# Attention with 32-wide heads in chunks of four heads, packed by way of DRAM, in a two-layer decoder

## What is computed

```python
q = q.reshape(B, S, 16, 32); k = k.reshape(B, M, 16, 32); v = v.reshape(B, M, 16, 32)
scores = einsum('bqhd,bkhd->bhqk', q, k) / sqrt(32)     # causal mask in the self-attentions
o = einsum('bhqk,bkhd->bqhd', softmax(scores), v)
```

## Time and profile before

| | us |
|---|---|
| median of three runs | 3690.84 (3683.32 to 3691.17) |
| the profiled execution | 3685.6, its span 3683.8 |
| granted TensorE clock over the span | 0.875 of full speed |
| busy PE / DVE / ACT / POOL | 3145.7 / 1262.7 / 966.9 / 835.5 |

### The profile page before, as it was taken

How to read it: one execution, slowest core, us unless ns; L and a number is a source line. 1 busy time by engine, 2 the same in 40 slices (tenths; PEclk the granted TensorE clock), 3 DMA queues, 4 the chain that set the end, 5 groups by cost and what they waited for, 6 DMA issues and landing times. The chain is left out here.

```text
span 3683.8 us, 40622 instructions
## 1 busy us (share of the span) xinstructions
PE 3145.7 (85%) x13163; PEld 1907.7 (52%) x13166; DVE 1262.7 (34%) x1863; ACT 966.9 (26%) x2096; POOL 835.5 (23%) x819
## 2 busy tenths in 40 slices
PE   7699796988549786888996998999999856999997
PEld 3354342333548633446885884555554442777773
DVE  3133334564401212435434225555552131111114
ACT  1133033554101012323332004444442000222220
POOL 2100001100121101002442104555553013212215
PEclk9656897999669986659998999999999957999998
DMA  2132203331059612313443433222220000999996
GB/s 77 44 80 58 88 12 76 71 76 31 28 183 325 225 62 58 81 47 123 140 142 114 133 99 132 71 71 72 71 71 20 24 18 16 340 334 338 338 332 190
DMA packets 320633, 442.93 MB, mean 120 GB/s; under 512 B 45502, under 2 KB 179622, under 8 KB 320520
## 3 DMA queue, kind: packets, MB, share of 16 engines
q1 hardware_dynamic: 290056, 370.14, 32.4%
q0 software_dynamic: 15488, 44.09, 3.8%
q10 hardware_dynamic: 14976, 27.27, 2.1%
HBM read 308.78 MB, written 75.58 MB: 104 GB/s over the span
## 5 line engine op out<-in xcount | busy, mean ns | idle before, releaser
L1360 PE MATMUL ps<-moe_blocks_xgt,moe_blocks_w 128*128 128x128 f32 (+1 forms) x3072 | 364.0, 277 | 8.8 <-DMA moe_blocks_b1s<-rb_cols 5.5
L510 ACT ACTIVATE normed<-ps 128x512 f32<-128x512 f32 (+3 forms) x512 | 247.5, 516 | 463.7 <-PE ps L452 293.3
L1360 PEld LDWEIGHTS ps<-moe_blocks_xgt,moe_blocks_w 128*128 128x128 f32 (+1 forms) x3072 | 348.9, 183 | 16.6 <-issue 15.0
L2239 POOL TENSOR_TENSOR normed<-normed,xa_core_rinv 128x257 f32<-128x257 f32 (+1 forms) x256 | 266.2, 1062 | 273.0 <-DVE xa_core_rinv L2170 273.0
L1342 PE MATMUL ps<-moe_blocks_w,moe_blocks_ht 128*128 128x512 f32 (+1 forms) x624 | 284.9, 593 | 0.0
L2206 ACT ACTIVATE normed<-ps,xa_core_nmax 128x257 f32<-128x257 f32 (+1 forms) x256 | 173.8, 685 | 321.8 <-DVE xa_core_nmax L2165 321.4
L2116 PE MATMUL ps<-xa_core_k,xa_core_q 128*128 128x512 f32 x512 | 242.3, 596 | 14.1 <-DVE xa_core_k L2155 11.4
L2165 DVE TENSOR_REDUCE xa_core_nmax<-ps 128x1 f32<-128x257 f32 (+1 forms) x256 | 164.5, 683 | 250.1 <-PE ps L2116 250.1
L1431 DVE COPY moe_blocks_y<-ps 128x512 f32<-128x512 f32 x104 | 72.0, 692 | 459.9 <-PE ps L1342 436.3
L2142 PE MATMUL ps<-xa_core_pt,xa_core_v 128*128 128x512 f32 x512 | 225.1, 592 | 0.7 <-DVE xa_core_pt L2178 0.7
L559 DVE TENSOR_REDUCE xa_core_nmax<-ps 128x1 f32<-128x1024 f32 x128 | 156.0, 1224 | 139.9 <-PE ps L432 139.9
(11 more groups left out here) (290 smaller groups left out, 5263.7 us busy)
## 6 DMA issues: line engine op xcount, KB each, us to landing
moe_blocks_w<-L_ffn_rw SPq DMA_DIRECT2D x80, 704.0 KB
moe_blocks_w<-L_ffn_rw SPq DMA_DIRECT2D x80, 512.0 KB
...
moe_y<-moe_blocks_y ACTq DMA_DIRECT2D x104, 256.0 KB
sa_core_packed<-sa_core_parts SPq DMA_DIRECT2D x384, 64.0 KB
k_raw<-xa_kq_raw SPq DMA_DIRECT2D x64, 256.0 KB, 2.0
v_rows<-normed SPq DMA_DIRECT2D x64, 256.0 KB
...
```

Of the source, the lines that this page charges most:

```text
L510: nc.scalar.activation(probs[:, e % RING, a:S], g.ps[:, 4 + h, a:S], ACT.Exp).then_inc(exp_done, 1)
L1360: mm = nc.tensor.matmul(g.ps[0:fn, 2 + s % 2 + 2 * half, f * P:(f + 1) * P], w1s[s][:, k, half * F + f0:half * F + f0 + fn], xgt[:, s % 2, ...
L2239: ins = nc.gpsimd.tensor_tensor(prob[:, n % PR, lo:hi], prob[:, n % PR, lo:hi], rinv[:, n % PR, m:m + 1].to_broadcast([P, hi - lo]), ALU.mult)
```

## The change

Only `attention_core` and the layout of v change. The work goes in 8 **chunks** i of four heads, one for each unit.

- **Packing.** `spill(i)` writes all parts of a unit to a DRAM buffer in one transfer (128 rows of 8 KB in sa, 12 KB in xa), and `pack(i)` waits for it and reads them back in six transfers, each 32 rows of 4 heads, into `pq` and `pk`. There are three slots in place of four for pairs. SP's order is `spill(i + 2)`, `pack(i + 2)`, `put_rows(i + 1)`; `put_rows` has two transfers for four heads. At the start the order is spill 0, spill 1, pack 0, pack 1.
- **High parts.** ACT makes those of unit i + 2 in step nkt / 2 of chunk i.
- **Values.** Four matmuls with 32 columns of v write the four quarters of PSUM bank 6, in the rows of the output, and four with 32 columns of ones write the sums to bank 7. `take` copies both banks straight to `total` and `ot`; `osb` and `lay` are gone. v is stored without ones, and the POOL memsets of ones in v are gone.
- **Order on PE.** A step makes scores of heads 0 and 1, up to three pieces of chunk i + 1 (eight pieces a chunk in sa, sixteen in xa), scores of heads 2 and 3, and the values of the step before. The pieces now run one chunk ahead. In sa two score matmuls stand together and then their two masks. Row maxima are turned in the last step of a chunk.
- **DVE.** `norm(i - 1)` comes after the piece PCS // 2 of chunk i + 1 and waits for `take` alone.

```diff
-    packed = st.sbuf("packed", [P, SLOTS, 2, 1 + KB, S], F32R)
+    pq = st.sbuf("pq", [P, SLOTS, HPC, S], F32R)
+    pk = st.sbuf("pk", [P, SLOTS, HPC, KB * S], F32R)
+    parts_dram = nc.dram_tensor(st.name + "_parts_rows", (NI, P, 2 + 2 * KB, S), F32, kind="Internal").ap()
...
+    nmax = st.sbuf("nmax", [P, 2, HPC * QB])
+    rows = st.sbuf("rows", [HPC * QB, 2, 2, P], F32R)
...
-            def pack(j):
-                u, s = j // 2, j % SLOTS
-                sp.wait_ge(low_done, 2 * u + 2)
-                if j >= SLOTS:
-                    sp.wait_ge(st_made, 2 * nkt * (j - SLOTS + 1))
-                t = parts[u % PB]
-                for h in range(2):
-                    a = (2 * (j % 2) + h) * DH
-                    for r, (qp, kp) in enumerate(TERMS):
-                        sp.dma_start(packed[r * DH:(r + 1) * DH, s, h, 0, :].bitcast(F32),
-                                     t[a:a + DH, qp, :].bitcast(F32)).then_inc(packed_in[s], 16)
-                        sp.dma_start(packed[r * DH:(r + 1) * DH, s, h, 1:1 + KB, :].bitcast(F32),
-                                     t[a:a + DH, 2 + KB * kp:2 + KB * (kp + 1), :].bitcast(F32)).then_inc(packed_in[s], 16)
-
...
+            def spill(i):
+                sp.wait_ge(low_done, 2 * i + 2)
+                sp.dma_start(parts_dram[i], parts[i % PB][:, :, :].bitcast(F32)).then_inc(spilled[i % 2], 16)
+
+            def pack(i):
+                s = i % SLOTS
+                sp.wait_ge(spilled[i % 2], 16 * (i // 2 + 1))
+                if i >= SLOTS:
+                    sp.wait_ge(st_made, HPC * nkt * (i - SLOTS + 1))
+                t = parts_dram[i].rearrange("(h p) a n -> p h a n", p=DH)
+                for r, (qp, kp) in enumerate(TERMS):
+                    sp.dma_start(pq[r * DH:(r + 1) * DH, s, :, :].bitcast(F32),
+                                 t[:, :, qp, :]).then_inc(packed_in[s], 16)
+                    sp.dma_start(pk[r * DH:(r + 1) * DH, s, :, :].bitcast(F32),
+                                 t[:, :, 2 + KB * kp:2 + KB * (kp + 1), :].rearrange("p h a n -> p h (a n)")
+                                 ).then_inc(packed_in[s], 16)
+
...
-            def lay(j):
-                i = j // 2
-                sp.wait_ge(taken, j + 1)
-                if j % 2 == 0 and i >= 1:
-                    sp.wait_ge(normed, i)
-                for h in range(2):
-                    a = (2 * (j % 2) + h) * DH
-                    val, ones = (3 if h else 0) * DH, (1 + h) * DH
-                    sp.dma_start(ot[a:a + DH, i, :], osb[val:val + DH, j % 2, :]).then_inc(spread[j % 2], 16)
-                    sp.dma_start(total[a:a + DH, :], osb[ones:ones + DH, j % 2, :]).then_inc(spread[j % 2], 16)
-
-            for j in range(SLOTS):
-                pack(j)
+                    sp.dma_start(pq[KR + n:KR + n + 1, i % SLOTS, :, :].bitcast(F32),
+                                 rows[:, i % 2, n, :].bitcast(F32)).then_inc(rows_in[i % 2], 16)
...
+            spill(0)
+            spill(1)
+            pack(0)
+            pack(1)
             put_rows(0)
-            for j in range(NP):
-                if j >= 1 and j + SLOTS - 1 < NP:
-                    pack(j + SLOTS - 1)
-                if j + 1 < NP:
-                    put_rows(j + 1)
-                if j >= 1:
-                    lay(j - 1)
-            lay(NP - 1)
-            for n in range(2):
-                sp.wait_ge(spread[n], 64 * NP // 2)
+            for i in range(NI):
+                if i + SLOTS - 1 < NI:
+                    spill(i + SLOTS - 1)
+                    pack(i + SLOTS - 1)
+                if i + 1 < NI:
+                    put_rows(i + 1)
...
                     for h in range(2):
-                        nc.tensor.matmul(g.ps[:, bank + h, 0:w], packed[0:KR, s, h, 0, n * P:(n + 1) * P],
-                                         packed[0:KR, s, h, 1, 0:w], start=True, stop=False)
-                        mm = nc.tensor.matmul(g.ps[:, bank + h, n * P:w], g.ident16[:, :], mask16[:, :], start=False,
+                        nc.tensor.matmul(g.ps[:, bank + h, 0:w], pq[0:KR, s, 2 * pair + h, qb * P:w],
+                                         pk[0:KR, s, 2 * pair + h, 0:w], start=True, stop=False)
+                    for h in range(2):
+                        mm = nc.tensor.matmul(g.ps[:, bank + h, qb * P:w], g.ident16[:, :], mask16[:, :], start=False,
                                               stop=True)
...
+                    mm = nc.tensor.matmul(g.ps[:, 4 + h % 2, a:S], pk[0:KR + 2, s, h, kb * P:(kb + 1) * P],
+                                          pq[0:KR + 2, s, h, a:S], start=True, stop=not causal)
+                    if not causal:
+                        mm.then_inc(st_made, 1)
...
-                for h in range(2):
-                    nc.tensor.matmul(g.ps[2 * h * DH:2 * (h + 1) * DH, 6 + j % 2, a:S],
-                                     v[:, j // (H // 2), kb, j % (H // 2), h:h + 2, :].rearrange("p a d -> p (a d)"),
-                                     probs[:, (e + h) % RING, a:S], start=(kb == 0),
-                                     stop=(kb == nkt - 1)).then_inc(pv_made, 1)
+                    for h in (2 * pair, 2 * pair + 1):
+                        nc.tensor.matmul(g.ps[:, 4 + h % 2, a:a + P], mask16[:, :], g.ident16[:, :], start=False,
+                                         stop=True).then_inc(st_made, 1)
+
+            def values(i, kb):
+                step, a = nkt * i + kb, start_of(kb)
+                b, c = divmod(i, KC)
+                pe.wait_ge(exp_done, HPC * step + HPC)
+                if kb == 0 and i >= 1:
+                    pe.wait_ge(taken, 2 * i)
+                for h in range(HPC):
+                    nc.tensor.matmul(g.ps[h * DH:(h + 1) * DH, 6, a:S], v[:, b, kb, c * P + h * DH:c * P + (h + 1) * DH],
+                                     probs[:, HPC * (step % STEPS) + h, a:S], start=(kb == 0), stop=(kb == nkt - 1))
+                for h in range(HPC):
+                    mm = nc.tensor.matmul(g.ps[h * DH:(h + 1) * DH, 7, a:S], g.ones[:, 0:DH],
+                                          probs[:, HPC * (step % STEPS) + h, a:S], start=(kb == 0), stop=(kb == nkt - 1))
+                mm.then_inc(pv_made, 1)
...
             turn(0)
-            for n in range(nkt):
-                piece(1, n)
             pe.wait_ge(early_ones_done, 1)
             pe.wait_ge(late_ones_done, 1)
-            for j in range(NP):
+            for i in range(NI):
                 for kb in range(nkt):
-                    scores(j, kb, 0)
-                    scores(j, kb, 1)
-                    if kb == 0 and j + 1 < NP:
-                        turn(j + 1)
+                    ahead = range(min(PCS, EACH * kb), min(PCS, EACH * (kb + 1))) if i + 1 < NI else ()
+                    if i == 0:
+                        for m in ahead:
+                            piece(i + 1, m)
+                    scores(i, kb, 0)
+                    if i > 0:
+                        for m in ahead:
+                            piece(i + 1, m)
+                    if kb == nkt - 1 and i + 1 < NI:
+                        turn(i + 1)
+                    scores(i, kb, 1)
                     if kb >= 1:
-                        values(j, kb - 1)
-                    elif j >= 1:
-                        values(j - 1, nkt - 1)
-                    if j + 2 < NP:
-                        piece(j + 2, kb)
-            values(NP - 1, nkt - 1)
+                        values(i, kb - 1)
+                    elif i >= 1:
+                        values(i - 1, nkt - 1)
+            values(NI - 1, nkt - 1)
...
-            def high_parts(u):
-                if u >= PB:
-                    for j in (2 * (u - PB), 2 * (u - PB) + 1):
-                        act.wait_ge(packed_in[j % SLOTS], PACK * (j // SLOTS + 1))
-                for x, hi in zip((qt, kt), high(u)):
-                    nc.scalar.activation(hi, x[:, u, :], ACT.Copy).then_inc(high_done, 1)
...
+            def high_parts(i):
+                if i >= PB:
+                    act.wait_ge(spilled[(i - PB) % 2], 16 * ((i - PB) // 2 + 1))
+                for x, hi in zip((qt, kt), high(i)):
+                    nc.scalar.activation(hi, x[:, i, :], ACT.Copy).then_inc(high_done, 1)
...
-            def take(j):
-                act.wait_ge(pv_made, 2 * nkt * (j + 1))
-                if j >= 2:
-                    act.wait_ge(spread[j % 2], 64 * (j // 2))
-                nc.scalar.activation(osb[:, j % 2, :], g.ps[:, 6 + j % 2, :], ACT.Copy).then_inc(taken, 1)
...
+                if step >= STEPS:
...
+            def take(i):
+                act.wait_ge(pv_made, nkt * (i + 1))
+                if i >= 1:
+                    act.wait_ge(normed, i)
+                nc.scalar.activation(total[:, :], g.ps[:, 7, :], ACT.Copy).then_inc(taken, 1)
+                nc.scalar.activation(ot[:, i, :], g.ps[:, 6, :], ACT.Copy).then_inc(taken, 1)
...
-            for j in range(NP):
```

(46 more changed lines are left out.)

195 lines of the change are left out of this document (87 added, 108 removed).

## The result

The changed kernel takes **3890.23 us** (median, 3887.95 to 3893.94) against 3689.86 us (3683.32 to 3691.17) for the kernel before, measured side by side: ratio **1.0548**, 95% interval 1.0529 to 1.0566. It is slower by 200 us where +135 was forecast, 5 us outside the range given. The profiled execution has a span of 3892.1 us.

A forecast was written before the change was run, and what follows sets the result against it. PE was taken to bound sa at 1.2 GHz, and PE with its order xa. The sa cores at 283.0 (+28.5, +32.0) and xa at 438.6 (+74.5) add +135 to 3685.6: 3820 us, range 3705 to 3885.

The forecast's parts named there:

- the chain: Between chunks: high parts, low parts, spill, pack and rows one after another, 20.7 us in xa and 15.6 in sa.
- the pack: Reading parts back from DRAM at 362 GB/s plus 2.7 us fixed: 9.1 us in xa, 6.9 in sa.
- the clock behind the wait: In xa, an idle stretch is followed by time at 1.2 GHz, adding 2 us to the period of 49.1.
- The 28.4 to the high parts: In xa, us from the start of a chunk to its high parts, with steps of 5.5 and norm 1.7.
- the 51.1 forecast: Period of a chunk in xa: 49.1 us plus 2 for slow clock, in place of 40.2 before.
- The start: First scores after the core's start: xa 53.3 us against 46.2 before; sa 27.6 against 38.3, a gain of 10.7.
- Its period: Period of a chunk in sa: 34.9 us, in place of 28.6 before.
- PE's work: A chunk's own work: xa 41.5 us against 40.2 steady; sa 27.5 at 1.2 GHz against 28.6, 17 at 2.4.
- rival 2: Values on PE: the four quarters don't run side by side, so values double; about 3990 us, chance 0.06.
- the loss of a quarter: Values on PE would take a quarter longer by the skill's factor of 2.38x for three tiles, not 3x.
- Rival 1: SP's issues bound sa and the chain is short, 13.5 us in sa, 18.5 in xa: 3667 us, chance 0.14.
- Rival 3: sa stays wholly at 1.2 GHz, period 37.1: 3855 to 3880 us, the forecast's upper end, within its chance of 0.76.

The follow-up runs named there:

- e1_early: The changed kernel with one condition altered, so high parts of unit i + 2 are made in step 0, not step nkt / 2: 3691.27 us, ratio 1.0004.
- the experiment on partitions: The changed kernel with pack's transfers over 96 partitions (3845.38 us), or mostly over 0 to 63 (3899.07 us) or 32 to 95 (3878.08 us).
- e6_turn: The changed kernel with parts made a chunk earlier, third pieces behind values, norm behind the last maximum, turn a step earlier: 3538.39 us, ratio 0.9630.

## Why the prediction was wrong

Direction, place and mechanism were right: slower, by a wait at each chunk's first scores, six times a core, since the parts were made too late for the round trip over DRAM. e1_early shows it as the cause, not only as an idle time: with the chain moved to the chunk's start, the wait in xa is 0.69 and the whole loss is gone, though 6 us of waiting stay in sa. What failed is the size of two terms: the pack, in xa and in sa, and the clock behind the wait, in xa.

- **`pack`, the failed step.** It was priced at 9.1 in xa and 6.9 in sa, with 0.8 for the rows behind it, by the 362 GB/s of the earlier trace rows. With the rows it took 13.97 (871.16 to 885.13) for 9.9, and 10.62 (289.69 to 300.31) for 7.7. 2.36 MB at 210 GB/s are 11.2. The rate of a transfer over 128 partitions was put on transfers over 32, the nearest row by direction but not by shape. The trace of the kernel before held a hint of the lower rate (663.00:666.00, shown with the experiment on partitions). The other links were right: high and low parts 5.3 (5.25 forecast) and 3.7 (3.7); spill 5.1 (5.5) and 3.9 (4.2).
- **The clock behind the wait in xa.** The 28.4 to the high parts were 33.1. Steps were as forecast at full clock (5.5), `norm` cost 1.9 (1.7 forecast); but the first step took 8.6 (827.65 to 836.26) and the matmuls behind the long stall 1.6 more. That is 4.7 a chunk, where 2 stood in the sum. The waits came out at 11.2 to 12.1 us in xa, forecast at 6 to 10.
- Together 4.1 + 2.7, less 0.4 at the spill, make a period of 57.5 for the 51.1 forecast. Six periods give 42 of xa's miss of 52 (490.4 measured, 438.6 forecast). The start gives 5.5 more (first scores 58.8 after the core's start, not 53.3), again packs at half the rate, and chunk 6 and the end 4.4.
- **sa was right partly by luck.** Its period, 35.2 to 36.5 from turn to turn, was forecast at 34.9, but of wrong parts: chain 18.25 for 15.6, time to the high parts 17.1 to 18.2 for 19.3. The start gained 4.6, not 10.7: first scores came 33.7 after the core's start, not 27.6. So the two cores came out 294.4 and 289.7 against 283.0.
- **PE's work was right.** Four quarters do run side by side: eight matmuls L455 in 1.06, eight L458 in 1.04 (0.88 and 0.98 between starts), 2.0 forecast. So rival 2 is out, and so is the loss of a quarter that the factor of the Trainium skill ("TensorE: Matmul & The Clock Gate", Part 3) would have made. A chunk of sa at 2.4 GHz was forecast at 17 and is 17.3 in e6_turn.
- **Rival 1** needed a period of sa under 31; it was 35 to 36. But the runs agree with what it said of SP: once the chain was out of the way, whole chunks of sa ran at 2.4 GHz in 17.3 us, with 9 issues a unit, where the 40 issues of before alone are 25. No run changed the issues alone, so this stays argued. The step that I didn't see is that the two effects can be had apart, by one condition.
- **Rival 3** didn't come: sa's granted clock was 0.64 and 0.66, above the 0.56 of the earlier trace rows in the first core.

The upper end of the range, 3885, held rival 3's clock but no price of the pack beyond. With the packs as measured the same sum gives 3820 + 6 x 4.1 + 12 x 2.9 = 3879, and some 15 more for the three starts. Rival 2's sum has a slip that changed nothing: 3820 + 78 + 100 is 3998, not 3990.
